# A six-layer transformer kernel on one core: constants multiplied in TensorE's first waits, an earlier load of the second chunk of x, and a new order on every engine

## The reference, cut to what matters

```
x = x + 0.5 * moe0(layernorm(x))      # MOE0_A: 16 experts, 128 -> 256 -> 128, all computed, top 2 gate
x = x + attn0(layernorm(x))           # ATT0: linear attention, sums over the sequence
x = x + 0.5 * moe0(layernorm(x))      # MOE0_B
x = x + 0.5 * moe1(layernorm(x))      # MOE1_A: 16 experts, 128 -> 128, relu, top 2 gate
x = x + attn1(layernorm(x))           # ATT1: causal linear attention, cumulative sums
x = x + 0.5 * moe1(layernorm(x))      # MOE1_B
```

## Time and profile before

| | us |
|---|---|
| median of 3 runs | 694.1 |
| lowest and highest run | 693.88, 695.51 |
| the profiled execution | 697.73 |
| its span, first to last instruction | 695.8 |
| PE busy in the span | 641.5 (92%) |
| DVE busy | 468.4 (67%) |
| ACT busy | 436.3 (63%) |
| POOL busy | 187.8 (27%) |
| mean granted TensorE clock | 0.969 |

### The profile page before, as it was taken

One profiled execution on the slowest core, in us unless ns is written; L12 is line 12 of the kernel. 1 busy time (PEld: TensorE's weight loads), 2 busy tenths in 40 slices (PEclk: granted clock), 3 DMA queues, 4 the chain that ended last, 5 costly groups with the idle time before them and its releaser, 6 DMA issues.

```text
span 695.8 us, 7583 instructions
## 1 busy us (share of the span) xinstructions
PE 641.5 (92%) x2361; PEld 408.2 (59%) x2361; DVE 468.4 (67%) x1063; ACT 436.3 (63%) x928; POOL 187.8 (27%) x132
## 2 busy tenths in 40 slices
PE   4999998999999899999999999999999967879784
PEld 3556564556556465676566666565766645555562
DVE  6588457634347955647799858879875577389542
ACT  4454455644446654697775495785489535988495
POOL 3120010200011101044251044051016252576465
PEclk9899999999999999999999999999999988999898
DMA  8842622155324213402133312204231000000000
GB/s 249 203 82 63 107 75 54 31 101 87 97 60 61 60 38 105 103 27 63 34 61 63 80 42 54 68 1 106 56 57 27 0 1 0 0 16 2 15 15 17
DMA packets 26737, 41.44 MB, mean 60 GB/s; under 512 B 1784, under 2 KB 9032, under 8 KB 26696
## 3 DMA queue, kind: packets, MB, share of 16 engines
q1 hardware_dynamic: 25128, 37.80, 24.9%
q10 hardware_dynamic: 1568, 3.15, 1.5%
HBM read 39.64 MB, written 1.31 MB: 59 GB/s over the span
## 4 chain that ended last, share of the span: by engine, by line
PE 67%; ACT 14%; DVE 11%; issue 5%; POOL 2%; DMA 0%; SPq 0%; POOLq 0%; ACTq 0%; DVEq 0%
PE py L1133 27%; PE ph L906 7%; PE ph L908 7%; PE ph L907 7%; ACT stage L551 7%; ACT bc L551 4%; PE ps L1041 2%; PE ps L1043 2%; PE ps L1042 2%; PE ph L1087 2%; DVE stage L760 1%; PE ps L1090 1%; PE py L1136 1%; ACT g L600 1%; PE ps L1091 1%
## 5 line engine op out<-in xcount | busy, mean ns | idle before, releaser
L600 ACT ACTIVATE g<-ph,b1col 128x512 f32<-128x512 f32 x256 | 172.3, 694 | 133.5 <-PE ph L908 121.1
L1133 PE MATMUL py<-hw,w2s 128*128 128x512 f32 x512 | 244.6, 601 | 1.5 <-DVE hw L866 1.5
L866 DVE TENSOR_TENSOR hw<-g,bc 128x1024 f32<-128x1024 f32 x125 | 161.6, 1301 | 86.9 <-ACT g L600 81.7
L1133 PEld LDWEIGHTS py<-hw,w2s 128*128 128x128 f32 x512 | 96.0, 192 | 77.6 <-issue 62.8
L906 PE MATMUL ph<-xbh,w1h 128*128 128x512 f32 x256 | 136.6, 534 | 0.6 <-ACT g L600 0.6
L388 POOL TENSOR_TENSOR rstd<-vare,mhalf 128x4 f32<-128x4 f32 x24 | 36.3, 1514 | 359.3 <-DVE vare L676 359.2
L551 ACT ACTIVATE stage<-ps,comb 128x128 f32<-128x128 f32 x384 | 107.2, 569 | 12.9 <-PE ps L1043 9.6
L908 PE MATMUL ph<-xbh,w1l 128*128 128x512 f32 x256 | 102.9, 402 | 0.0
L907 PE MATMUL ph<-xbl,w1h 128*128 128x512 f32 x256 | 102.6, 401 | 0.0
L448 POOL TENSOR_TENSOR stage<-stage 128x1024 f32<-128x1024 f32 x24 | 57.3, 2389 | 67.3 <-ACT stage L551 67.3
L906 PEld LDWEIGHTS ph<-xbh,w1h 128*128 128x128 f32 x256 | 49.4, 193 | 31.1 <-issue 21.5
(11 more groups left out here) (200 smaller groups left out, 847.8 us busy)
## 6 DMA issues: line engine op xcount, KB each, us to landing
bc<-comb_rows SPq DMA_DIRECT2D x31, 1024.0 KB, 8.4
stage<-in_L_ffn_W_dram SPq DMA_DIRECT2D x4, 512.0 KB, 6.8
X<-in_L_attn_x_dram SPq DMA_DIRECT2D x4, 256.0 KB, 10.4
out_dram<-X SPq DMA_DIRECT2D x4, 256.0 KB, 2.3
comb_rows<-combT SPq DMA_DIRECT2D x8, 32.0 KB, 6.5
bc<-comb_rows SPq DMA_DIRECT2D x1, 256.0 KB, 3.7
side<-in_L_attn_wq_dram SPq DMA_DIRECT2D x1, 64.0 KB, 7.0
side<-in_L_attn_wk_dram SPq DMA_DIRECT2D x1, 64.0 KB, 8.3
```

Of the source, the lines that this page charges most:

```text
L600: nc.scalar.activation(g[:, s % 2, h, 0:w], ph[:, (HC * s + h) % RING_PH, 0:w], ACT.Gelu, bias=b1col[:, HC * e + h:HC * e + h + 1]).then_i ...
L866: V.tensor_tensor(hw[:, s % RING_HW, :, 0:w], g[:, s % 2, :, 0:w], gates.unsqueeze(1).to_broadcast([P, HC, w]), ALU.mult).then_inc(hw_read ...
L1133: ins = T.matmul(py[:, 0:cols], w2s[:, w], hw[:, s2 % RING_HW, h, 0:cols], start=e2 == 0 and h == 0, stop=False)
```

## The change

Three things are changed. PE multiplies a tile of ones by itself (128x128, float32, into a bank of `ps` that nothing reads) ten times ahead of the first transpose, four times ahead of the first layer norm's transposes and five times behind them. SP issues chunk 1 of X behind the first quarter of W1 and `b1`, and no longer behind all weights. And the strings for PE, ACT, DVE and POOL are new; they hold the same numbers of steps of each stream.

```diff
@@ SP, first loads @@
                 if i == 0:
                     sp.dma_start(b1row[:, :], b1.rearrange("e (c p) -> (e c) p", p=P)).then_inc(w_in["b1"], 16)
+                    sp.dma_start(X[:, col(1)].rearrange("p (t d) -> p t d", d=D), x_t[:, tiles(1), :]).then_inc(x_in[1], 16)
...
-            for c in range(1, NCH):
+            for c in range(2, NCH):
                 sp.dma_start(X[:, col(c)].rearrange("p (t d) -> p t d", d=D), x_t[:, tiles(c), :]).then_inc(x_in[c], 16)
@@ PE @@
+            def keep_running(n):
+                for _ in range(n):
+                    T.matmul(ps[:, 2, 0:P], ones[:, :], ones[:, :], start=True, stop=True)
+
             def w1_(l, c):
+                keep_running(10)
                 pe.wait_ge(w_in["b1"], 16)
...
             def ln(l, c):
                 light_bank(("ln", l, c))
+                if (l, c) == MAIN[0]:
+                    keep_running(4)
                 pe.wait_ge(light["xn"], nth_light("xn", l, c))
...
                 ins.then_inc(light["xt_ps"], 1)
+                if (l, c) == MAIN[0]:
+                    keep_running(5)
                 yield
@@ TURNS, the start of DVE's string @@
-    "DVE": ("m k4 l2 h l h2 l h l3 h l m6 l6 m2 l m2 l m2 l2 m2 h m4 h4 m4 h2 m14 l2 m2 l m4 l m2 h2 m4 h l m4 l m2 l m2 l3 m12 l "
+    "DVE": ("l2 h l3 h l3 h m l k m3 l h k m3 l h l m8 l m l k m2 l m h m2 l m h m h k m l m4 h m h m h m4 l m h m3 l4 m3 h m4 h m8 "
```

## The result

The changed kernel takes 684.92 us, the median of four runs (682.37 to 685.95), against 694.81 for the kernel before on the same chip (693.88 to 698.48). The ratio is 0.984, with a 95% interval from 0.981 to 0.987. By the medians 9.9 us are gone, by the ratio 11 (9.2 to 12.9). The two profiled executions, 697.73 before and 685.95 after (spans 695.8 and 684.0), differ by 11.8.

A forecast was written before the change was run, and what follows sets the result against it. Three limits: DVE's wait for chunk 1 and PE's clock in the head, PE's work from 45 to 550 us, mutual waits in the tail. Head 7.0 + main 0 + tail 4.3 = 11.3 off 694.1 gives 682.8 us, range 676.5 to 689.5.

The forecast's parts named there:

- the head: Up to the fourth pair of `py` products, at 42.69 us before: 7.0 us gained, ends 5.0 and 8.5.
- the main stream: The stretch from 45 to 550 us, PE busy nearly throughout: 0 gained, ends 3 us gained and 2 lost.
- The constants: Products of ones on PE in the head: zero net, some 0.9 us gained at the router's products; ends 2.0 lost, 1.1 gained.
- DVE's chain: In the head: router from 12.1 to 15.5 us, `comb` 3.0 us earlier, no DMA wait for chunk 1, `xn` at 20.4.
- on PE the transposed gates, the copy on ACT and L922 end near 19.8, earlier than that: In the head: these end before `xn` at 20.4 us, so the first `py` starts at 23.6 instead of 26.95.
- a granted clock of 0.5 for more than 7 us in the head: PE's low clock in the head, named beforehand as a profile sign that the forecast is wrong.
- the waits of the main stream close too: Rival: 3 us gained there and both leads at their upper ends, 675.7 us, more likely 678; chance 0.10.
- The tail: Behind the main stream: 4.3 us gained, ends 0 and 6.9; first relus 2.3 sooner, ACT's waits 2.0 less.
- ACT gaps closed: In the tail: seven groups in a row close half of 4.0 us waits or copies in ACT's 32 groups, 2.0 gained.
- The slower one: Rival: MOE1's reductions ahead of gate products make PE wait 1.7 us a tile, 20 in all, 703 us; chance 0.07.
- The change does not shorten the head: Rival: chunk 1 still lands late, about 2 us of the chain's gain left, 688 to 692 us; chance 0.08, shared.
- Head only: Rival: the finer order gives nothing behind 45 us, or ATT1 of chunk 2 cancels the tail's gain; 687.1 us; chance 0.20.

The follow-up runs named there:

- the bundle: Kernel before, with chunk 3's router ahead of ATT1's second tile on PE and DVE, its exponential earlier on ACT, first `kvl` earlier on DVE: 696.01 us, ratio 1.001.

## Why the prediction was right, and where it wasn't

The forecast was 682.8 us (676.5 to 689.5), the result 684.92. The sum of 11.3 stands against 9.9 by the medians, 11 by the ratio and 11.8 in the profiles. Its terms were off by more than that, in both directions, and that they cancel is luck: the head was taken 2.6 us too high, the main stream 1.4 to 2.7 too low.

**The constants** did up to the router what was written: no cost at the transposes (8.16 against 8.10) and 1.5 us gained at the first 512-column product behind the router (11.56 against 13.07; the forecast had 0.9).

**DVE's chain** was right to 0.4 us: router from 11.74 to 15.54 (12.1 to 15.5 forecast), no wait for the DMA, `xn` of chunk 1 done at 20.34 (20.4).

**The head** was sized wrong: 4.4 us instead of 7.0, below the lower end of 5.0. The step that failed is "on PE the transposed gates, the copy on ACT and L922 end near 19.8, earlier than that". They ended at 23.4, because the clock fell at 17.0, and the first `py` came at 28.40 instead of 23.6. I had priced a fall with L922's 2.4 us only; it lasted 10.2 us and slowed the `ph` products too. What brought it was the change's own success: the earlier PE was done, the longer it waited for `comb`, 2.38 us. The run with ten more ones gives 34.93 at the mark, 7.8 us in front of before, between the 7.0 taken and the 8.4 said for a clock that stays up; its first `py`, at 25.05, is still 1.45 us behind the forecast, with the clock low from 20 to 23.4. So the chain of the sum was right in the main, and the clock was the term sized wrong. The 4.4 and the 7.8 carry the spread of the head, 1.7 us between profiles of one order. The text's own sign for that, a granted clock of 0.5 for more than 7 us in the head, is what the profile shows.

**The main stream** was set at 0, with 3 gained as end, and gave 1.4 in the two profiles. 2.7 is the difference where neither kernel's clock fell near 110 us (512.6 with the old order, 509.9 with the new one). It is the rival "the waits of the main stream close too", at a smaller price. Which steps of the new order brought it wasn't tried. PE's waits from 45 to 550 us show where they lie: the seven longest add up to 10.0 us before and 8.7 after. The three largest of each (us in total, times, longest), before, then after:

```profile
PE ps L1012 <- DVE side L763: 3.9, 3, 1.9
PE pl L989 <- DVE comb L728: 1.7, 3, 0.7
PE ps L1058 <- DVE X L767: 1.6, 2, 0.8
```

```profile
PE ps L1031 <- DVE side L773: 2.6, 2, 1.9
PE pl L980 <- DVE xn L692: 2.0, 3, 1.0
PE py L1152 <- DVE hw L876: 1.5, 2, 1.3
```

**The tail** was set at 4.3 and gave 6.0 in the two profiles. No other pair gives as much: `comb` and rest together are 136.9 to 139.0 us in the table's four profiles with the old tail and 133.0 to 135.7 in the five with the new one and without ones in the tail, 3.4 apart in the mean. So the size was about right, and the reason wrong. `comb` came 5.9 us closer to the main stream's end, not 2.9. I had given this to the router's move ahead of ATT1's second tile; alone that costs 5 us. With the exponential's place on ACT and that of the first `kvl` it costs nothing and gains nothing, and 4.4 of the 5.5 us lie in steps that I had not read in the strings: ATT1's first products on PE, POOL's product ahead of the root, and `xbl` ahead of `a1.4`, by the timelines and not by runs of their own. The 2.0 for "ACT gaps closed" is not there: the 32 groups took 37.1 us instead of 38.2, but they started 1.2 behind `comb`, behind a `kvh` that waited for products which PE did at 1.2 GHz, and the rest of the span is equal to 0.1 us in this pair and some 2 us longer in the others.

**The rivals.** The slower one had PE waiting for the gate product behind MOE1's reductions. PE's whole wait for `hw` from 45 to 550 us is 1.5 us (the last row above), 1.1 before. "The change does not shorten the head" falls with DVE's timeline; the order alone is just that case, and its 690.94 lies in that rival's 688 to 692. "Head only" falls with the order alone and with the runs that exchange the tails.

**The clock's price** by the runs: nineteen ones alone changed nothing (0.999, 0.996 to 1.002), and 45 more in PE's waits brought 4.7 us, 0.7% of 684.92, in a kernel whose mean granted clock is 0.974. The rule quoted from the Trainium skill (TensorE: Matmul & The Clock Gate, Part 1), a ramp penalty under 1% of a span, agrees with both numbers, though most of the 45 stand against later falls of the clock and not against its first rise.

## What to carry to other kernels

An engine that waits earlier and longer can lose in clock what it won in time: behind every step that is pulled forward, look whether PE's new wait is filled, and try products into a free bank there (3.4 us at the head mark, 4.7 us by the medians with the tail's). A step that is moved ahead must take along what it waits for on every other engine: the router moved on PE and DVE alone, with its exponential left behind on ACT, lost 5 us. Compare POOL's order too, even if its steps are few. A difference of two profiles can hold 2 us that no other pair shows; read the same distance from several kernels that share the order. And a cut or a move of an order should be read as the instructions' order on all engines before its time is believed.

## What was unexpected in the hardware

The clock fell behind busy time too. In the run with ten more ones PE was busy 4.84 of 5 us up to 20 us, the last 2.6 of them with the products of L937, which use 16 of 128 rows, and at 20 us the granted clock fell to 0.5 for 3.4 us. In the kernel before it fell at 24.9, while the same products ran. That these products are the reason isn't shown.

Identical instructions ran at the low clock for different times: the head of the kernel before for 6.8 us in one profile, and for 3.4 in the profile of the router moved alone, whose head has the same order.

DVE's `xn` of four 128-column pieces takes 1.11 us with POOL idle (557.57) and 2.21 or 2.73 beside a POOL add of 1.95 us (564.74 before, 563.14 in the bundle). POOL's own root took 1.91 us beside DVE's `kvl` in the kernel before and 1.01 in the kernel after. The POOL add and `xn` don't wait for each other, and yet their meeting cost 1.1 us in front of `comb` before and 1.6 in the bundle.
